# Turning row sums and final pair sums with 64-column matmuls on both halves of TensorE

## The reference

```python
h = maximum(layernorm(x), 0)                       # 8192 x 64
x = x + adj @ (h * (u >= 0.1) / 0.9)               # layer 1
h = maximum(layernorm(x), 0)
x = x + adj @ (h @ W) + b                          # layer 2
```

## Time and profile before

| | |
|---|---|
| median of 3 runs | 967.2 us (967.04 to 967.74) |
| the profiled execution | 967.56 us, span 965.8 us |
| TensorE | busy 927.2 us (96%), clock 1.00 throughout |
| turns of rows | 16, 128 MATMUL records, 17.7 us |
| turns of pairs | 8, 64 MATMUL records, 9.0 us |
| DMA | 350.96 MB, mean 363 GB/s |
| DVE, ACT, POOL | 15%, 2%, 3% of the span |

### The profile page before, as it was taken

The page is one execution under the profiler, slowest core; times in us unless marked ns, Lnnn a source line. Parts: engine busy times, 40 slices in busy tenths (PEclk is TensorE's granted clock), DMA queues, the critical chain, the costliest instruction groups (busy, mean ns, idle before and its releaser), DMA issues.

```text
span 965.8 us, 10106 instructions
## 1 busy us (share of the span) xinstructions
PE 927.2 (96%) x4288; PEld 317.7 (33%) x4288; DVE 142.0 (15%) x301; ACT 23.7 (2%) x52; POOL 33.7 (3%) x31
## 2 busy tenths in 40 slices
PE   2888999999999999999999989999999999999998
PEld 0122233333333333333433334333333333333334
DVE  6310101101010101010020101100200100100223
ACT  3000000000000000000000000000000000000000
POOL 7600000000000000000000000000000000000000
PEclk9999999999999999999999999999999999999999
DMA  9999999999999899989999899899999999999981
GB/s 330 409 410 409 409 410 409 409 409 365 412 369 378 300 412 355 383 274 400 373 315 352 286 321 386 317 372 396 305 348 409 360 375 396 368 374 409 409 350 66
DMA packets 98347, 350.96 MB, mean 363 GB/s; under 512 B 10960, under 2 KB 11504, under 8 KB 98304
## 3 DMA queue, kind: packets, MB, share of 16 engines
q1 hardware_dynamic: 98208, 350.27, 94.9%
q0 software_dynamic: 96, 0.07, 0.1%
HBM read 348.19 MB, written 2.10 MB: 363 GB/s over the span
## 4 chain that ended last, share of the span: by engine, by line
PE 81%; DMA 14%; SPq 4%; issue 0%; DVE 0%; DVEq 0%
PE row_sums L467 44%; PE banks L473 35%; DMA blocks<-in_adj 14%; SPq L280 3%; PE turned L511 1%; PE turned L522 1%; SPq L273 0%; SPq L274 0%; DVE rows L429 0%; DVEq L195 0%
## 5 line engine op out<-in xcount | busy, mean ns | idle before, releaser
L467 PE MATMUL row_sums<-blocks,features 128*64 128x512 f32 x2048 | 689.3, 599 | 34.0 <-DVE features L378 18.6
L473 PE MATMUL banks<-blocks,features 128*64 128x512 f32 x2048 | 673.5, 593 | 1.2 <-DMA blocks<-in_adj 1.2
L467 PEld LDWEIGHTS row_sums<-blocks,features 128*64 128x64 f32 x2048 | 208.2, 137 | 397.6 <-issue 308.5
L473 PEld LDWEIGHTS banks<-blocks,features 128*64 128x64 f32 x2048 | 213.5, 137 | 228.4 <-issue 226.7
L419 DVE TENSOR_TENSOR acc<-acc,banks 128x512 f32<-128x512 f32 (+1 forms) x87 | 59.7, 687 | 714.3 <-PE banks L473 641.9
L342 ACT ACTIVATE sums_sb<-row_sums 128x512 f32<-128x512 f32 x16 | 9.6, 597 | 777.5 <-PE banks L473 432.6
L393 DVE TENSOR_TENSOR rows<-rows,turned 128x256 f32<-128x256 f32 x16 | 6.8, 422 | 88.7 <-PE turned L511 88.7
L511 PEld LDWEIGHTS turned<-fold,sums_sb 128*128 128x128 f32 x128 | 15.5, 191 | 13.0 <-issue 13.0
L308 POOL TENSOR_SCALAR acc<-acc 128x512 f32<-128x512 f32 (+1 forms) x9 | 18.8, 2092 | 0.8
L511 PE MATMUL turned<-fold,sums_sb 128*128 128x64 f32 x128 | 17.7, 281 | 0.0
L522 PEld LDWEIGHTS turned<-pair_w,acc 128*128 128x128 f32 x64 | 7.7, 191 | 5.7 <-issue 5.7
(11 more groups left out here) (25 smaller groups left out, 43.3 us busy)
## 6 DMA issues: line engine op xcount, KB each, us to landing
blocks<-in_adj SPq DMA_DIRECT2D x656, 512.0 KB, 7.5
out<-rows SPq DMA_DIRECT2D x8, 256.0 KB, 2.0
rows<-in_x SPq DMA_DIRECT2D x7, 256.0 KB, 6.3
acc<-in_u SPq DMA_DIRECT2D x7, 256.0 KB, 6.3
rows<-in_x SPq DMA_DIRECT2D x2, 128.0 KB, 2.3
acc<-in_u SPq DMA_DIRECT2D x2, 128.0 KB, 2.6
pair_w<-in_w POOLq DMA_DIRECT2D x2, 16.0 KB, 3.7
bias<-in_b POOLq DMA_DIRECT2D x1, 32.0 KB, 6.0
```

Of the source, the lines that this page charges most:

```text
L467: return nc.tensor.matmul(row_sums[at, s % 2, :], features[:, k * TILES + j, 0:D], tile_of(parts, j), start=first and t.n == row_first[s][ ...
L473: return nc.tensor.matmul(banks[at, t.sum.bank, :], features[:, t.k * TILES + j, D:2 * D], tile_of(parts, j), start=t.n == t.sum.first and ...
```

## The change

Both turns do each tile of 128 nodes as two matmuls of 64 stationary columns, one for each half of the array: nodes 0 to 63 of the tile to partitions 0 to 63, nodes 64 to 127 to partitions 64 to 127. The moving operands (`fold`, `pair_w`), the results, the waits and the semaphore counts stay as they are. The program's matmuls in a turn go from 4 to 8.

```diff
                 for j in range(TILES):
-                    done = nc.tensor.matmul(turned[:, s % 2, j * D:(j + 1) * D],
-                                            sums_sb[:, s % 2, j * P:(j + 1) * P], fold[:, :], start=True, stop=True)
+                    for half in range(2):
+                        at, nodes = slice(half * D, (half + 1) * D), j * P + half * D
+                        done = nc.tensor.matmul(turned[at, s % 2, j * D:(j + 1) * D],
+                                                sums_sb[:, s % 2, nodes:nodes + D], fold[:, :], start=True, stop=True)
                 done.then_inc(turned_ready, 1)
 ...
                 for j in range(TILES):
-                    done = nc.tensor.matmul(turned[:, n % 2, j * P:(j + 1) * P],
-                                            acc[:, p, j * P:(j + 1) * P], pair_w[:, :], start=True, stop=True)
+                    for half in range(2):
+                        at, nodes = slice(half * D, (half + 1) * D), j * P + half * D
+                        done = nc.tensor.matmul(turned[at, n % 2, j * P:(j + 1) * P],
+                                                acc[:, p, nodes:nodes + D], pair_w[:, :], start=True, stop=True)
                 done.then_inc(turned_ready, 1)
```

## The result

The changed kernel takes **956.19 us** (median of 4 runs, 954.59 to 956.99) against 967.12 (4 runs of the kernel before): ratio 0.9884, 95% interval 0.9867 to 0.9901. That is 10.9 us less; 956.0 was forecast. Run once more in a later session it gave 955.38, ratio 0.9884 (0.9867 to 0.9900).

A forecast was written before the change was run, and what follows sets the result against it. DMA paces the kernel until about 200 us, TensorE after that. Row turns 8.8 plus pair turns 2.4 give 11.2 us less, from the median 956.0 us; range 953.0 to 963.5, its own 955.0 to 957.5, forecast chance 54%.

The forecast's parts named there:

- Row turn, 1.18 to 0.45: Each row turn: eight passes per half at 0.056 us, gaps gone, 0.73 us less; twelve count, 8.8 us.
- Pair turn, 1.24 to 0.87: Each pair turn: eight passes at 0.109 us, 0.36 us less; with the last two, 2.4 us in all.
- The gaps belong to the shape: Before and behind each turn: gaps of 0.09 to 0.1 us come from the shape change and go; bounds 0 to 0.19 left.
- Rival C: Around each turn: the gaps stay, nothing of the 0.19 us goes; 3.4 us less gained, 959.4; chance 8%.
- The early four count for nothing: Row turns before 200 us, where DMA sets the pace: their saving becomes waiting, nothing gained, 2.9 us as the other end.
- The last two pair turns, 0.2 less: End of the kernel: with no step between or behind them they save one gap and one open load, 0.2 us together.
- A: Inside each turn: a load with its MATMUL keeps the 0.111 pitch whatever its columns; 11.5 us more, 978.7; chance 7%.
- B: Inside each turn: instruction issue paces the burst at 0.056 us per MATMUL; only 6.3 us saved, 960.9; chance 10%.
- D: Inside each turn: load and stream don't overlap within a half for small matmuls; 3.4 us saved, 963.8; chance 5%.
- G: Inside each turn: the halves take turns, each pass at full speed; about 967.7, no change; chance 3%.
- E: Between 200 and 560 us: DMA takes back what the seven row turns save, 5.1 us; 961.1; chance 10%.
- F: Before 200 us: the savings of the four early row turns count after all; 953.1; chance 3%.

The follow-up runs named there:

- the extra matmul: Changed kernel with one more matmul at the head of each row turn: with 128 stationary columns 962.34 us, as two of 64 columns 955.77 us.
- the quarters: Changed kernel with pair turns cut into 64 rows x 64 columns, sixteen matmuls over four quarters of the array: 955.76 us, ratio 0.9885.

## Why the prediction was right

956.0 was forecast and 956.19 measured, by the steps that were named.

**What bounds.** Right. The seven turns between 200 and 560 us alone bring 4.5 us, the four before 200 us 0.8 with an interval that touches zero.

**Row turn, 1.18 to 0.45.** It takes 0.46: the pitch of a pass is 0.058, not 0.056, and the gaps and open loads are gone. 12 x 0.72 = 8.6 was expected of the row turns alone with that pitch, 8.3 measured.

**Pair turn, 1.24 to 0.87.** 0.87 in the trace; 2.1 us by the kernel with this part alone, 2.4 in the prediction.

**The gaps belong to the shape.** Argued before from a single row; shown now by the extra matmul (0.10 on either side with 128 columns, none with two of 64) and by the quarters. Rival C is out. In that single row, 1.89 for 16 loads, the prediction forgot the length of the last load: 15 x 0.111 + 0.19 = 1.86, and 0.03 are left for the semaphore. Its reading, no gap, stands.

**The early four count for nothing.** Nearly. The fifth turn comes 0.47 us earlier in the new trace, of 2.9 saved, but 0.40 later in the second profile of the changed kernel, so this number alone says little. Much of its spread is there from the start: the first matmul starts between 17.52 and 19.26 us in the thirteen profiles (18.33 before, 18.48 after). Counted from it, the last step before the fifth turn is over after 209.2 to 210.2 us in the seven profiles whose early turns take 0.46, and after 210.1 to 210.3 in the three that leave these turns as they were: some 0.4 us of 2.9 came through on average. The block for which TensorE stood at 194.90 is used in the new kernel at

```profile
194.43 0.20 PEld L467 LDWEIGHTS row_sums<-blocks,features 128*64 128x64 f32 x4 [0.85 <-DMA blocks<-in_adj]
```

with nearly the same idle time before it (0.81), so in this trace the data themselves came earlier; why, no run shows. I had forecast 2 to 3 us more of waits before 200 us; the two profiles of the changed kernel show 1.1 and 1.6 more than 11.7. A MATMUL record of 0.59 lasts 0.16 beyond its stream, and waits hide behind it, so this view undercounts them.

**The last two pair turns, 0.2 less.** Wrong, with a size that does not matter here: in the old trace the last MATMUL starts 2.34 us after the last block step's start, in the new one 2.32. The wait for DVE's addition took the place of what was saved. The prediction said that nothing on DVE changes; it had looked for waits of block matmuls alone, and not of the last turn.

**The rivals.** A and B fall with the turn of 0.46 us: sixteen loads and sixteen MATMULs in it are 0.0145 per instruction, so neither a fixed pitch of 0.111 nor an issue at 0.056 per instruction paces the burst. The Trainium skill, "TensorE: Matmul & The Clock Gate", section "Part 2: What happens when you issue a matmul", has about 62 ns per MATMUL for decoding in microcode; the sixteen MATMULs here come at 29 ns each, and in quarters 32 of them in 0.47 us at 15 ns, so that figure does not bind here. Whether these were decoded ahead, while the block steps streamed, no run shows. D falls with the pitch of 0.058 for a load and a stream of 0.054 each, G with 16 passes in the time of 8. E is out by the seven turns alone, F by the early four.

What was lucky: whole runs of one kernel differ by 2 to 3 us, and the match within 0.2 us is closer than the method is; the match per turn, 0.01 to 0.02 us, is not luck. Two things that no turn touches go far to explain the spread: the start of the first matmul (17.5 to 19.3 us) and the waits for blocks near 430 and 555 us (1.2 to 4.0). If both are taken off the profiled span, 944.2 us are left before, and less by 2.2 with the pair turns alone, 5.0 with the seven turns, 8.7 with the row turns alone, and 11.4 and 12.0 in the two profiles of the whole change. The turns by themselves give 2.2, 5.0, 8.6 and 10.8. With the early four alone it is 1.4 less, so what these are worth is known only as a small part of 2.9.

## What to carry to other kernels

If the bulk of the matmuls runs in two halves of the array, a few full-width ones between them cost more than their own passes: two shape changes with their open weight loads were 0.40 us here, as much as nearly a whole step. Keep small matmuls in the shape of their surroundings, and issue them alternating between the halves. Count such savings only where TensorE sets the pace, and look for what is late next behind the last instance, where nothing follows that could hide it.

## What was not expected of the hardware

In the profiled execution of the kernel with the extra 128-column matmul TensorE waited 0.74 and then 2.32 us for blocks, and the granted clock fell. TensorE in stretches of 2 us (PE busy, PEld, DVE, ACT, POOL, clock, DMA share, GB/s):

```profile
558.00:560.00 2.00, 0.85 (x4) 0.00 (x0) 0.00 (x0) 0.00 (x0) 0.00 (x0) 1.00 0.97 234
560.00:562.00 2.00, 0.82 (x4) 0.34 (x6) 0.00 (x0) 0.00 (x0) 0.00 (x0) 1.00 0.87 348
562.00:564.00 2.00, 2.00 (x8) 0.61 (x6) 0.00 (x0) 0.00 (x0) 0.00 (x0) 0.50 0.91 371
564.00:566.00 2.00, 2.00 (x10) 0.58 (x8) 0.00 (x0) 0.00 (x0) 0.00 (x0) 0.65 0.49 152
```

Steps there are 0.85 apart (562.16, 563.02, 563.88 in the timeline) in place of 0.43. Four of them, from 562.16 to 565.50, ran at 1.2 in place of 2.4 GHz and took 3.3 us where 1.7 would have done. The kernel before, with a longest wait of 1.8 us in the same place and one of 0.62 ahead of it, kept its clock. The execution took 964.85 us against a median of 962.34. One run of the kernel with the seven turns also had a mean granted clock of 0.998; it took 964.08 us, the other four 960.33 to 961.61. So a wait for data can cost more than itself, 1.6 us here behind one of 2.32; how long a wait it takes was not tested.
